# Two regions in DRAM for the second layer's experts, and scatters without a wait between tiles

## Chip, cores and metric

The kernel runs on one core of one Trainium2 chip. The metric is the device time of one execution in microseconds (us). Several executions are timed; one further execution is recorded by the hardware profiler, and all rows here come from that one.

## What is computed

The program is a two-layer transformer on x of 16 batches x 512 tokens x 256 features in fp32. Each layer scales and shifts a normalised x, adds an attention branch, and then a branch with experts. The change is in the last part, the experts of the second layer (`_L1_ffn_ref`):

```python
def _moe(x, gate_w, w1, w2):            # T = 8192 tokens, 8 experts, top 2
    probs = jax.nn.sigmoid(x_flat @ gate_w)
    _, sel = jax.lax.top_k(probs, TOP_K)
    w_topk = jnp.take_along_axis(probs, sel, axis=1)
    w_topk = w_topk / (jnp.sum(w_topk, axis=-1, keepdims=True) + 1e-06)
    ...  # each (token, choice) gets a slot in its expert, up to a capacity of 2560
    h = jax.nn.gelu(jnp.einsum('ecd,edf->ecf', padded_x, w1), approximate=False)
    out_padded = jnp.einsum('ecf,efd->ecd', h, w2)...
    out_w = out_rep * w_topk.reshape(-1)[:, None]
    return out_w.reshape(T, TOP_K, D).sum(axis=1).reshape(B, S, D)

src = _rmsnorm(x + _gqa(x, ...), norm1_w)
src = src + _moe(src, gate_w, w1, w2)
return _rmsnorm(src, norm2_w)           # times a gate, added to x, is the output
```

## The kernel before

The program is one long sequence of blocks: set-up, the first layer's attention (`local_attention_block`), its experts on two batches' rows (`routed_experts_block`), the second layer's attention and routing (`mixer_block`), and the second layer's experts (`experts_block`). Each block has one instruction list per engine, and semaphores set the order. SyncE issues nearly all DMAs from one in-order list, so whatever waits there holds back every later load and store. GpSimd issues the indirect DMAs (scatters) from its own list.

Ahead of `experts_block`, `mixer_block` has written the normalised rows `src` to DRAM (`src_dram`, 8192 rows of 256; the profile calls it src_rows) and has scattered a copy of each row, with its two routing entries, into the slots of its experts (`padded_dram`). A row there is 260 numbers: 256 features, the token's number (column D), the slot of its first choice (D+1), and the two weights.

`experts_block` then works through 71 tiles (NTILEX) of 256 rows, each with one expert. Per tile i:

- SyncE loads the rows xe (260 KB), w1 and w2 (512 KB each), the weights three tiles ahead of their use, each as soon as the tile that holds the buffer is through with it (`up_done`, `y_done`).
- TensorE, iteration i: transposes of tile i+2 (L4135), up-projection of tile i+1 (L4147), down-projection of tile i (L4159). Each projection is 16 matmuls. The up-projection waits for VectorE's copy of the transposed rows.
- ScalarE applies gelu.
- VectorE, iteration i, in this order: `copy_rows(i+2)` (L4040) copies the transposed rows out of PSUM; `place_rows(i)` waits until the scatters of tile i-3 have landed, since they read the same buffer of `place`, then makes the row numbers `place` (L4049) and the weights (L4052 to L4059); in some iterations a step of a finished batch; `copy_out(i)` (L4065) writes the weighted output rows `ye`. The instructions run in order, so a wait in `place_rows(i)` holds back `copy_out(i)` and `copy_rows(i+3)`.
- GpSimd issues two indirect DMAs (L4013), 128 rows each, that add `ye` into `src_dram` at `place`. Ahead of the first it waits until both scatters of tile i-1 have landed, since a token's two choices may lie in neighbouring tiles and would be added to the same row. The second also waits for `up_done` of tile i+2.

The tiles are sorted so that batch b is complete after tile 4b+10. With it, in the iterations that follow: SyncE loads its 512 rows back (`load_src`, L3946; for the last batch in two halves, L3950) at i = 4b+12; VectorE takes statistics (`stats`, L4078) at i = 4b+13, the reciprocal square root (`root`, many small steps of 128x4) at 4b+14, scales by gate and norm (`scale`, L4092) at 4b+15; GpSimd adds the result to x (`add_x`, L4001) after the scatters of tiles 4b+15 and 4b+16; SyncE stores x (`store`, L3956) at i = 4b+18. The last batch is finished on VectorE alone (L4118, L4125).

Parts of `padded_dram` are zero-filled in the first layer's attention, by stores of SyncE, two for each batch (`clear`, L758).

Of the kernel before, what the change touches and what calls it, by code (L numbers as in the profile page):

```python
# [5 lines left out]
F32 = mybir.dt.float32  # L6
# [4 lines left out]
ALU = mybir.AluOpType  # L11
AX = mybir.AxisListType

P = 128
D = 256
C = D // P
B = 16
S = 512
NT = S // P
T = B * S  # L20
# [620 lines left out]
        sp.dma_start(m.n1w[:, :], I["L1_ffn_norm1_w"].partition_broadcast(P)).then_inc(m.mixer_w_in, 16)  # L641


def local_attention_block(nc, m, I, mods_dram, padded_dram, sorted_dram):

# [5 lines left out]
    with nc.cleanup_on_exit(), ctx:  # L651
        def sem(name):
# [24 lines left out]

        expert_norm = (m.xn_rows[:, :, :], kT[:, 0, :, :].rearrange("p c s -> p (c s)")[:, 0:NT * ROW]
                       .rearrange("p (t d) -> p t d", d=ROW))
        ZERO_STORES = 2 * B + 1 + (NTILE0 + ZR - 1) // ZR  # L680
# [50 lines left out]
        def _(sp):  # L731
# [23 lines left out]
            def clear(b):  # L755

                for j in range(2):
                    sp.dma_start(padded_dram[bass.ds(b * (E * CAP // B) + j * (P * ZR), P * ZR), :]  # L758
                                 .rearrange("(p r) d -> p (r d)", p=P), no_rows).then_inc(zero_filled, 16)

            sp.wait_ge(m.rows_out, 16)
            load_norm_rows(0)
# [3090 lines left out]
def experts_block(nc, m, I, mods_dram, src_dram, padded_dram, out):  # L3853
# [10 lines left out]
    with nc.cleanup_on_exit(), ctx:  # L3864
# [12 lines left out]
        src = sb("src_e", [P, 2, NT, D])  # L3877
        second = sb("second", [P, RT])
        change = sb("change", [P, RT])
        weight = sb("weight", [P, WB, RT])  # L3880
# [26 lines left out]
            return m.x[:, b * (NT * D) + h * (2 * D):b * (NT * D) + (h + 1) * (2 * D)]  # L3907

        def pair(b, h):
            return src[:, b % 2, 2 * h:2 * h + 2, :].rearrange("p t d -> p (t d)")  # L3910

        block = ctx.enter_context(nc.Block())

# [1 line left out]
        def _(sp):  # L3915
# [26 lines left out]
            def load_src(b):  # L3942
                rows_sent(complete(b))
                if b >= 2:
                    sp.wait_ge(x_ready, 2 * (b - 1))
                sp.dma_start(src[:, b % 2, :, :], src_dram[b * S:(b + 1) * S, :].rearrange("(t p) d -> p t d", p=P))\  # L3946
                    .then_inc(src_in[b % 2], 16)

            def load_last(b, h):
                sp.dma_start(src[:, b % 2, 2 * h:2 * h + 2, :],  # L3950
                             src_dram[b * S + h * (2 * P):b * S + (h + 1) * (2 * P), :].rearrange("(t p) d -> p t d", p=P))\
                    .then_inc(src_in[h], 16)

            def store(b, h):
                sp.wait_ge(x_ready, 2 * b + h + 1)
# [41 lines left out]
        @block.gpsimd  # L3997
        def _(pool):
            def add_x(b, h):
                pool.wait_ge(z_ready, b * NT + 2 * h + 2)  # L4000
                pool.tensor_tensor(x_half(b, h), x_half(b, h), pair(b, h), ALU.add).then_inc(x_ready, 1)  # L4001

            for i in range(NTILEX):
                pool.wait_ge(place_ready, i + 1)
                pool.wait_ge(ye_ready, i + 1)
                for t in range(RT):
                    if t == 0 and i:

                        pool.wait_ge(sent[(i - 1) % WB], 16 * RT * ((i - 1) // WB + 1))

                    if t == 1 and i + 2 < NTILEX:
                        pool.wait_ge(up_done, 2 * (i + 2) + 1)
                    pool.indirect_dma_start(src_dram,  # L4013
                                            bass.IndirectOffsetOnAxis(ap=place[:, i % WB, t:t + 1], axis=0),
                                            ye[:, i % WB, t, :], None, bounds_check=T - 1, oob_is_err=False,
                                            compute_op=ALU.add)\
                        .then_inc(sent[i % WB], 16)
                if i >= 15 and i % 4 in (3, 0):
                    add_x((i - 15) // 4, (i - 15) % 4)
            for h in range(2):  # L4020
# [13 lines left out]
        def _(dve):  # L4034
# [8 lines left out]
            def place_rows(i):  # L4043
                u = i % WB
                dve.wait_ge(x_in[u], 16 * (i // WB) + 16)

                if i >= WB:
                    dve.wait_ge(sent[u], 16 * RT * (i // WB))
                dve.tensor_copy(place[:, u, :], xe[:, i % XB, :, D]).then_inc(place_ready, 1)  # L4049

                dve.wait_ge(weight_ready, 4 * i)
                dve.scalar_tensor_tensor(out=second[:, :], in0=xe[:, i % XB, :, D + 1], scalar=m.row_x[:, i:i + 1],  # L4052
                                         in1=m.own[:, :], op0=ALU.subtract, op1=ALU.not_equal).then_inc(weight_ready, 1)
                dve.tensor_tensor(change[:, :], xe[:, i % XB, :, D + 3], xe[:, i % XB, :, D + 2], ALU.subtract)\
                    .then_inc(weight_ready, 1)
                dve.wait_ge(weight_ready, 4 * i + 2)
                dve.tensor_tensor(change[:, :], change[:, :], second[:, :], ALU.mult).then_inc(weight_ready, 1)
                dve.wait_ge(weight_ready, 4 * i + 3)
                dve.tensor_tensor(weight[:, u, :], change[:, :], xe[:, i % XB, :, D + 2], ALU.add).then_inc(weight_ready, 1)  # L4059
# [13 lines left out]
                dve.tensor_tensor(gate_norm[:, b, :], gate_norm[:, b, :], n2w[:, :], ALU.mult).then_inc(gates_ready, 1)  # L4073

            def stats(b):
                dve.wait_ge(src_in[b % 2], 16 * (b // 2) + 16)
                for t in range(NT):
                    step(dve.bn_stats(m.bn[:, t, :], src[:, b % 2, t, :]))  # L4078

            def root():  # L4080
                step.settle()
# [7 lines left out]
                emit_rsqrt(dve, step, m, m.rstd[:, 0:NT], m.meanvar[:, 0:NT, 1], EPS_NORM, NT)  # L4089

            def scale(b, t, done):
                done(dve.scalar_tensor_tensor(out=src[:, b % 2, t, :], in0=src[:, b % 2, t, :], scalar=m.rstd[:, t:t + 1],  # L4092
                                              in1=gate_norm[:, b, :], op0=ALU.mult, op1=ALU.mult))

            def scaled(ins):
# [17 lines left out]
                copy_out(i)  # L4113
            for t in range(NT):
                scale(B - 2, t, scaled)
            for t in range(NT):
                dve.wait_ge(src_in[t // 2], 16 * (B // 2 + 1 - t // 2))
                step(dve.bn_stats(m.bn[:, t, :], src[:, (B - 1) % 2, t, :]))  # L4118
            root()
            dve.wait_ge(x_ready, 2 * (B - 1))  # L4120
            for h in range(2):
# [52 lines left out]
def build_program(nc, I, out):  # L4174
# [6 lines left out]
    src_dram = nc.dram_tensor("src_rows", (T, D), F32, kind="Internal").ap()  # L4181
    ctx = ExitStack()
    with ctx:
        m = allocate(nc, ctx)
        with ExitStack() as lists:
            with ExitStack() as mixer:
                with ExitStack() as experts:
                    first_layer_lists(nc, m, experts)
                    with ExitStack() as local:
                        local_weights(nc, m, local)  # L4190
                        setup_block(nc, m, I, mods_dram)
                        expert_buffers(nc, m, experts)
                        local_attention_block(nc, m, I, mods_dram, padded_dram, sorted_dram)
# [28 lines left out]
```

## Time and profile before

| | us |
|---|---|
| median of 3 runs | 3264.03 |
| lowest, highest | 3258.34, 3270.96 |
| the profiled execution | 3275.82 |
| its span on the core | 3274.1 |

```profile
PE 3027.8 (92%) x20262; PEld 1870.4 (57%) x20262; DVE 2182.0 (67%) x6629; ACT 1589.0 (49%) x3518; POOL 1203.4 (37%) x1522
```

This line of the page gives each engine's busy time, its share of the span, and its instructions: PE is TensorE's matmuls, PEld its weight loads, DVE VectorE, ACT ScalarE, POOL GpSimd; SP or SPq is SyncE with its queue. Busy shares are averages over stages with different limits, so the stage of the change has to be read by itself: which engine is busy without a gap, and where one has gaps, what ended each wait. In a timeline a row gives the start, the time busy, the engine, the line of the kernel, what it wrote from what, and in brackets how long the engine had been idle before it and who released it.

### The profile page before, as it was taken

To read this page: it belongs to the slowest core of one execution; us is meant where nothing else is said; L and a number is where in the kernel's file an instruction comes from. 1 tells how busy PE (TensorE), PEld (TensorE's weight loads), DVE (VectorE), ACT (ScalarE), POOL (GpSimd) and SP (SyncE) were. 2 spreads that over 40 slices of the span, in tenths; PEclk is the share of its full clock that TensorE was granted. 3 is DMA by queue.
4 is the path that set the end of the run, shared out by engine and by line. 5 is a ranking of instruction groups with operands and counts; after the bars stand their busy time and mean duration, and the time that the engine had idled before them with its cause. 6 is when DMAs were issued, how large, how long until landed. Compare 5 with 4: busy or idle time off the path is not lost. (4 is left out here: it accounts for less than half of the span.)

```text
span 3274.1 us, 59846 instructions
## 1 busy us (share of the span) xinstructions
PE 3027.8 (92%) x20262; PEld 1870.4 (57%) x20262; DVE 2182.0 (67%) x6629; ACT 1589.0 (49%) x3518; POOL 1203.4 (37%) x1522
## 2 busy tenths in 40 slices
PE   6799999999998986999999999999998859998896
PEld 3566667667665653344444444444443348887785
DVE  6777777777762224788888888888887633544445
ACT  3466565565641113566667677676665511111110
POOL 2123232232333114234444444444443224444445
PEclk8899999999999997899999999999999979999998
DMA  8110010100125961122222222222222138878884
GB/s 272 5 49 27 26 50 26 50 25 26 50 68 168 310 210 48 54 62 74 75 75 75 74 74 74 75 76 76 76 75 71 52 102 218 246 212 230 225 219 131
DMA packets 269401, 338.17 MB, mean 103 GB/s; under 512 B 43952, under 2 KB 218659, under 8 KB 269105
## 3 DMA queue, kind: packets, MB, share of 16 engines
q1 hardware_dynamic: 240112, 296.62, 28.7%
q0 software_dynamic: 28464, 34.71, 5.3%
q8 instruction: 170, 2.79, 0.4%
q10 hardware_dynamic: 544, 3.15, 0.3%
q14 instruction: 111, 0.90, 0.1%
HBM read 225.77 MB, written 113.95 MB: 104 GB/s over the span
## 5 line engine op out<-in xcount | busy, mean ns | idle before, releaser
L2841 DVE TENSOR_REDUCE negmax<-psum 128x1 f32<-128x512 f32 x1024 | 667.6, 683 | 163.1 <-PE psum L3394 149.5
L2459 ACT ACTIVATE pT<-psum 128x512 f32<-128x512 f32 x1024 | 576.1, 595 | 291.7 <-PE psum L3423 199.9
L3394 PE MATMUL psum<-k_stack,q_stack 96*128 96x512 bf16 x1024 | 359.1, 389 | 20.8 <-DVE negmax L2841 17.9
L3423 PE MATMUL psum<-q_stack,k_stack 99*128 99x512 bf16 x1024 | 361.4, 384 | 15.9 <-ACT pT L2459 9.8
L4013 POOL DMA_INDIRECT src_rows<-ye,place x142 | 224.6, 1582 | 329.6 <-DVE place L4049 178.3
L4030 ACT ACTIVATE actT_x<-psum 128x512 f32<-128x512 f32 x142 | 84.8, 597 | 480.9 <-PE psum L4147 467.9
L940 ACT ACTIVATE probs<-probs,negmax 128x256 f32<-128x256 f32 x512 | 252.8, 495 | 123.4 <-DVE negmax L1031 121.8
L4147 PE MATMUL psum<-xT_x,w_x 128*128 128x256 f32 x1136 | 266.3, 389 | 30.9 <-DVE xT_x L4040 30.3
L3437 PE MATMUL psum<-pT,v_tile 128*32 128x512 f32 x2048 | 269.5, 610 | 1.0 <-ACT pT L2459 1.0
L4159 PE MATMUL psum<-w_x,actT_x 128*128 128x256 f32 x1136 | 256.6, 379 | 0.0
L4147 PEld LDWEIGHTS psum<-xT_x,w_x 128*128 128x128 f32 x1136 | 215.9, 195 | 62.7 <-DVE xT_x L4040 34.5
L1031 DVE CUSTOM_DVE_ANT_0 probs<-psum,band_mask 128x256 f32<-128x256 f32 x512 | 181.4, 420 | 104.7 <-PE psum L1304 104.0
L849 POOL TENSOR_TENSOR x<-x,scaled 128x256 f32 (+1 forms) x64 | 46.7, 729 | 525.4 <-DVE scaled L1092 525.4
L4159 PEld LDWEIGHTS psum<-w_x,actT_x 128*128 128x128 f32 x1136 | 215.8, 190 | 29.3
L1368 PE MATMUL psum<-w,actT 128*128 128x256 f32 x1024 | 231.4, 379 | 1.3 <-ACT actT L957 0.8
L1362 PE MATMUL psum<-x2T,w 128*128 128x512 f32 x512 | 228.9, 601 | 1.0 <-DVE x2T L1082 1.0
L3394 PEld LDWEIGHTS psum<-k_stack,q_stack 96*128 96x128 bf16 x1024 | 97.4, 98 | 210.6 <-DVE negmax L2841 130.9
L3423 PEld LDWEIGHTS psum<-q_stack,k_stack 99*128 99x128 bf16 x1024 | 99.3, 98 | 198.9 <-ACT pT L2459 107.2
L1368 PEld LDWEIGHTS psum<-w,actT 128*128 128x128 f32 x1024 | 193.1, 190 | 33.6 <-issue 6.2
L1362 PEld LDWEIGHTS psum<-x2T,w 128*128 128x128 f32 x512 | 99.3, 194 | 113.3 <-issue 110.0
L2272 POOL DMA_INDIRECT padded<-src,scatter_idx x128 | 125.4, 980 | 93.2 <-DVE scatter_idx L2987 56.5
L957 ACT ACTIVATE actT<-psum,b 128x512 f32<-128x512 f32 x128 | 87.9, 687 | 133.5 <-PE psum L1362 133.5
(402 smaller groups left out, 5588.3 us busy)
## 6 DMA issues: line engine op xcount, KB each, us to landing
w_x<-in_L_ffn_w_dram SPq DMA_DIRECT2D x142, 512.0 KB
w_e<-in_L_ffn_w_dram SPq DMA_DIRECT2D x46, 1024.0 KB, 7.0
q_stacks<-q_part SPq DMA_DIRECT2D x192, 128.0 KB
q_stack<-q_stacks SPq DMA_DIRECT2D x64, 384.0 KB, 4.4
padded<-w_e SPq DMA_DIRECT2D x32, 650.0 KB, 6.2
xe<-padded SPq DMA_DIRECT2D x71, 260.0 KB
gate_rows<-mods SPq DMA_DIRECT2D x66, 256.0 KB, 3.4
x<-in_L_attn_x_dram SPq DMA_DIRECT2D x16, 512.0 KB, 8.3
```

The costliest lines, as they stand in the source:

```text
L940: ins = act.activation(probs[:, h, :], probs[:, h, :], ACT.Exp, bias=negmax[:, h:h + 1], scale=-1.0, accum_out=zsum[:, t % 2, h:h + 1])
L1031: ins = dve.tensor_tensor_reduce(probs[:, h, :], bank(m, j)[:, i * 2 * P:(i + 1) * 2 * P], m.band_mask[:, variant, :], scale=-1.0, scalar= ...
L1362: mm = pe.matmul(bank(m, at), m.w1_0[:, c, f * P:(f + 1) * P], x2T[:, c, :], start=(c == 0), stop=(c == C - 1))
L1368: mm = pe.matmul(bank(m, at)[:, 0:D], actT[:, f, t * P:(t + 1) * P], m.w2_0[:, f, :], start=(f == 0), stop=(f == NF0 - 1))
L2459: act.activation(pT[:, 4 * (s % 2) + r, :], bank(m, 2 + n % 2), ACT.Exp, scale=float(DHQ) ** -0.5)\
L2841: dve.tensor_reduce(negmax[:, p // REP, h:h + 1], bank(m, max_bank(b, 16 * g + p)), AX.X, ALU.max, negate=True).then_inc(max_read, 1)
L3394: pe.matmul(bank(m, max_bank(b, 16 * g + p)), q_stack[0:K_SCORE, h, t * P:(t + 1) * P], k_stack[0:K_SCORE, g, :], start=True, stop=True).t ...
L3423: pe.matmul(bank(m, 2 + n % 2), k_stack[:, g, kc * P:(kc + 1) * P], q_stack[:, REP * g + r, :], start=True, stop=True).then_inc(sT_done, 1)
L3437: mm = pe.matmul(bank(m, VB)[VW * r:VW * (r + 1), :], v_tile[:, par, kc, g, :], pT[:, 4 * (s % 2) + r, :], start=(kc == 0), stop=(kc == NT ...
L4013: pool.indirect_dma_start(src_dram, bass.IndirectOffsetOnAxis(ap=place[:, i % WB, t:t + 1], axis=0), ye[:, i % WB, t, :], None, bounds_che ...
L4147: mm = pe.matmul(bank(m, 2 * (i % 2) + h)[:, (f % 2) * ROWS_X:(f % 2 + 1) * ROWS_X], w1[:, i % WB, c, f * P:(f + 1) * P], xT[:, i % 2, c, ...
L4159: mm = pe.matmul(bank(m, 4 + i % 2)[:, t * D:(t + 1) * D], actT[:, i % 2, f, t * P:(t + 1) * P], w2[:, i % WB, f, :], start=(f == 0), stop ...
```

## The change

- `src_dram` gets 2 x 8192 rows. The upper half takes the second choices. It is zero-filled in the first layer's attention by one more store per batch in `clear` (512 rows, 512 KB), and the count that readers of the zeros wait for (`ZERO_STORES`) grows by 16.
- `place` is now the token's number plus 8192 where this slot is not that of the first choice. It is made by a multiply-add on VectorE after `second`, in place of a copy ahead of it.
- No row of either half gets more than one addition, and GpSimd's wait between the scatters of successive tiles is taken out. The wait for `up_done` ahead of the second scatter stays, and so does that of `place_rows(i)` for tile i-3.
- `load_src` and `load_last` load both halves, so each load becomes two DMAs of the former size; the buffer `src` doubles.
- `stats` first adds the second half to the first (two additions of 128x512 per batch), also for the last batch.

```diff
@@ local_attention_block: clear @@
                 for j in range(2):
                     sp.dma_start(padded_dram[...], no_rows).then_inc(zero_filled, 16)
+                sp.dma_start(src_dram[bass.ds(b * S + T, S), :].rearrange("(p r) d -> p r d", p=P),
+                             no_rows.rearrange("p (r d) -> p r d", d=ROW)[:, 0:NT, 0:D]).then_inc(zero_filled, 16)
@@ experts_block: SyncE, load_src @@
                 rows_sent(complete(b))
                 if b >= 2:
                     sp.wait_ge(x_ready, 2 * (b - 1))
-                sp.dma_start(src[:, b % 2, :, :], src_dram[b * S:(b + 1) * S, :].rearrange("(t p) d -> p t d", p=P))\
-                    .then_inc(src_in[b % 2], 16)
+                for k in range(TOPK):
+                    sp.dma_start(src[:, b % 2, k, :, :],
+                                 src_dram[k * T + b * S:k * T + (b + 1) * S, :].rearrange("(t p) d -> p t d", p=P))\
+                        .then_inc(src_in[b % 2], 16)
@@ experts_block: GpSimd @@
                 for t in range(RT):
-                    if t == 0 and i:
-
-                        pool.wait_ge(sent[(i - 1) % WB], 16 * RT * ((i - 1) // WB + 1))
-
                     if t == 1 and i + 2 < NTILEX:
                         pool.wait_ge(up_done, 2 * (i + 2) + 1)
                     pool.indirect_dma_start(src_dram,
                                             bass.IndirectOffsetOnAxis(ap=place[:, i % WB, t:t + 1], axis=0),
-                                            ye[:, i % WB, t, :], None, bounds_check=T - 1, oob_is_err=False,
+                                            ye[:, i % WB, t, :], None, bounds_check=TOPK * T - 1, oob_is_err=False,
                                             compute_op=ALU.add)\
@@ experts_block: VectorE, place_rows @@
                     dve.wait_ge(sent[u], 16 * RT * (i // WB))
-                dve.tensor_copy(place[:, u, :], xe[:, i % XB, :, D]).then_inc(place_ready, 1)
-
                 dve.wait_ge(weight_ready, 4 * i)
...
                 dve.wait_ge(weight_ready, 4 * i + 2)
+                dve.scalar_tensor_tensor(out=place[:, u, :], in0=second[:, :], scalar=float(T), in1=xe[:, i % XB, :, D],
+                                         op0=ALU.mult, op1=ALU.add).then_inc(place_ready, 1)
@@ experts_block: VectorE, stats @@
-                dve.wait_ge(src_in[b % 2], 16 * (b // 2) + 16)
+                dve.wait_ge(src_in[b % 2], 16 * TOPK * (b // 2 + 1))
+                for h in range(2):
+                    step(dve.tensor_tensor(pair(b, h), pair(b, h), src[:, b % 2, 1, 2 * h:2 * h + 2, :]
+                                           .rearrange("p t d -> p (t d)"), ALU.add))
+                step.settle()
@@ experts_block: VectorE, last batch @@
-            for t in range(NT):
-                dve.wait_ge(src_in[t // 2], 16 * (B // 2 + 1 - t // 2))
-                step(dve.bn_stats(m.bn[:, t, :], src[:, (B - 1) % 2, t, :]))
+            for h in range(2):
+                dve.wait_ge(src_in[h], 16 * TOPK * (B // 2 + 1 - h))
+                step(dve.tensor_tensor(pair(B - 1, h), pair(B - 1, h), src[:, (B - 1) % 2, 1, 2 * h:2 * h + 2, :]
+                                       .rearrange("p t d -> p (t d)"), ALU.add))
+                step.settle()
+                for t in (2 * h, 2 * h + 1):
+                    step(dve.bn_stats(m.bn[:, t, :], src[:, (B - 1) % 2, 0, t, :]))
```

## Rows read from the trace of the kernel before

**Rows 1.** Windows of the experts' stage: us, busy of each engine, PEclk, DMA share, GB/s.
```profile
2693.80:2892.40 198.60, 198.60 (x976) 174.97 (x975) 81.41 (x311) 32.25 (x54) 85.71 (x56) 1.00 0.86 230
2892.40:3245.20 352.80, 321.94 (x1523) 278.81 (x1521) 174.24 (x618) 50.15 (x84) 165.01 (x108) 0.98 0.78 213
3245.20:3274.10 28.90, 0.02 (x1) 0.00 (x0) 14.24 (x51) 0.00 (x0) 12.82 (x9) 0.55 0.23 73
```

**Rows 2.** Timeline of TensorE: start us, us, engine line op, tiles, count, [idle before].
```profile
2690.33 3.62 PE L4159 MATMUL psum<-w_x,actT_x 128*128 128x256 f32 x16
...
2841.14 3.62 PE L4147 MATMUL psum<-xT_x,w_x 128*128 128x256 f32 x16
...
2848.48 3.62 PE L4147 MATMUL psum<-xT_x,w_x 128*128 128x256 f32 x16
...
2928.00 6.56 PE L4147 MATMUL psum<-xT_x,w_x 128*128 128x256 f32 x16 [3.42 <-DVE xT_x L4040]
...
3238.15 7.07 PE L4159 MATMUL psum<-w_x,actT_x 128*128 128x256 f32 x32
```

**Rows 3.** Waits, 2700 to 3240: engine line waited for: us in total, times, longest.
```profile
DVE place L4049 <- DMA src_rows<-ye,place: 144.6, 35, 6.3
...
PE psum L4147 <- DVE xT_x L4040: 30.3, 14, 3.7
```

**Rows 4.** Timeline of GpSimd in a stalled stretch.
```profile
2923.99 1.83 POOL L4001 TENSOR_TENSOR x<-x,src_e 128x512 f32<-128x512 f32 x1
...
2929.40 1.81 POOL L4013 DMA_INDIRECT src_rows<-ye,place  x1 [0.30 <-issue]
2939.28 1.55 POOL L4013 DMA_INDIRECT src_rows<-ye,place  x1 [8.07 <-issue]
2941.14 1.55 POOL L4013 DMA_INDIRECT src_rows<-ye,place  x1 [0.30 <-issue]
```

**Rows 5.** Timeline of VectorE in the same stretch.
```profile
2923.41 2.44 DVE L203 SCALAR_TENSOR_TENSOR rstd<-newton,rstd 128x4 f32<-128x4 f32 x1
...
2937.83 0.17 DVE L4049 CAST place<-xe 128x2 uint32<-128x2 f32 x1 [6.26 <-DMA src_rows<-ye,place]
...
2944.95 0.17 DVE L4049 CAST place<-xe 128x2 uint32<-128x2 f32 x1 [4.78 <-DMA src_rows<-ye,place]
```

**Rows 6.** Waits of the queue of SyncE, 2700 to 3240.
```profile
SPq L3956 <- POOL x L4001: 83.6, 12, 9.4
```

**Rows 7.** Timeline around the load of batch 2, without stalls.
```profile
2842.00 0.37 SPq L3946 DMA_DIRECT2D src_e<-src_rows  x1
...
2849.31 1.41 DVE L4078 BATCH_NORM_STATS2 bn<-src_e 128x6 f32<-128x256 f32 x4 [6.28 <-DMA src_e<-src_rows]
...
2851.41 0.68 DVE L4040 COPY xT_x<-psum 128x512 f32<-128x512 f32 x1
```

**Rows 8.** Chain that ended last: start us, us, what.
```profile
3257.85 2.71 DMA src_rows<-ye,place
...
3260.61 2.69 DMA src_e<-src_rows
...
3268.69 0.69 DVE x L4125
```

**Rows 9.** DMA in 40 equal slices of 2693.8 to 2892.4.
```profile
GB/s 174 211 267 221 157 272 175 227 245 234 178 243 227 216 219 202 235 204 223 329 204 288 163 213 213 330 204 280 277 160 222 353 178 320 255 165 152 282 309 194
```

**Rows 10.** Groups of instructions, 2700 to 3240: line, engine, op, shapes, count, busy, mean ns.
```profile
L4052 DVE SCALAR_TENSOR_TENSOR second<-xe,row_x,own_x 128x2 f32<-128x2 f32 x68 | 14.7, 216 | 0.0
```

**Rows 11.** Timeline of GpSimd at the end of the first layer's attention.
```profile
943.25 2.78 POOL L857 TENSOR_TENSOR xn<-xn,gate_rows 128x256 f32<-128x256 f32 x4 [25.46 <-DMA gate_rows<-mods]
...
971.30 0.73 POOL L849 TENSOR_TENSOR x<-x,scaled 128x256 f32<-128x256 f32 x1 [4.75 <-DVE scaled L1092]
```

**Rows 12.** Timeline around the last tile.
```profile
3250.45 0.88 DVE L4065 TENSOR_SCALAR ye<-psum,weight 128x256 f32<-128x256 f32 x2
...
3255.99 1.55 POOL L4013 DMA_INDIRECT src_rows<-ye,place  x1 [1.97 <-DMA src_rows<-ye,place]
```

More of the change, by code:

```diff
@@ L641, in load_mixer_weights, with local_attention_block @@
         sp.dma_start(m.n1w[:, :], I["L1_ffn_norm1_w"].partition_broadcast(P)).then_inc(m.mixer_w_in, 16)
-def local_attention_block(nc, m, I, mods_dram, padded_dram, sorted_dram):
+def local_attention_block(nc, m, I, mods_dram, padded_dram, sorted_dram, src_dram):
     ctx = ExitStack()
@@ L679, in local_attention_block @@
                        .rearrange("p (t d) -> p t d", d=ROW))
-        ZERO_STORES = 2 * B + 1 + (NTILE0 + ZR - 1) // ZR
+        ZERO_STORES = 2 * B + 1 + (NTILE0 + ZR - 1) // ZR + B
         second_s = sem("a_second_modulation_steps")
@@ L3876, in experts_block @@
         gate_norm = sb("gate_norm", [P, B, D])
-        src = sb("src_e", [P, 2, NT, D])
+        src = sb("src_e", [P, 2, TOPK, NT, D])
         second = sb("second", [P, RT])
@@ L3909, in pair @@
         def pair(b, h):
-            return src[:, b % 2, 2 * h:2 * h + 2, :].rearrange("p t d -> p (t d)")
+            return src[:, b % 2, 0, 2 * h:2 * h + 2, :].rearrange("p t d -> p (t d)")
         block = ctx.enter_context(nc.Block())
@@ L3945, in load_src @@
                     sp.wait_ge(x_ready, 2 * (b - 1))
-                sp.dma_start(src[:, b % 2, :, :], src_dram[b * S:(b + 1) * S, :].rearrange("(t p) d -> p t d", p=P))\
-                    .then_inc(src_in[b % 2], 16)
+                for k in range(TOPK):
+                    sp.dma_start(src[:, b % 2, k, :, :],
+                                 src_dram[k * T + b * S:k * T + (b + 1) * S, :].rearrange("(t p) d -> p t d", p=P))\
+                        .then_inc(src_in[b % 2], 16)
             def load_last(b, h):
-                sp.dma_start(src[:, b % 2, 2 * h:2 * h + 2, :],
-                             src_dram[b * S + h * (2 * P):b * S + (h + 1) * (2 * P), :].rearrange("(t p) d -> p t d", p=P))\
-                    .then_inc(src_in[h], 16)
+                for k in range(TOPK):
+                    at = k * T + b * S + h * (2 * P)
+                    sp.dma_start(src[:, b % 2, k, 2 * h:2 * h + 2, :],
+                                 src_dram[at:at + 2 * P, :].rearrange("(t p) d -> p t d", p=P)).then_inc(src_in[h], 16)
             def store(b, h):
@@ L4075, in stats @@
             def stats(b):
-                dve.wait_ge(src_in[b % 2], 16 * (b // 2) + 16)
+                dve.wait_ge(src_in[b % 2], 16 * TOPK * (b // 2 + 1))
[3 more added lines that the diff above has]
+                step.settle()
                 for t in range(NT):
-                    step(dve.bn_stats(m.bn[:, t, :], src[:, b % 2, t, :]))
+                    step(dve.bn_stats(m.bn[:, t, :], src[:, b % 2, 0, t, :]))
             def root():
@@ L4091, in scale @@
             def scale(b, t, done):
-                done(dve.scalar_tensor_tensor(out=src[:, b % 2, t, :], in0=src[:, b % 2, t, :], scalar=m.rstd[:, t:t + 1],
+                done(dve.scalar_tensor_tensor(out=src[:, b % 2, 0, t, :], in0=src[:, b % 2, 0, t, :], scalar=m.rstd[:, t:t + 1],
                                               in1=gate_norm[:, b, :], op0=ALU.mult, op1=ALU.mult))
@@ L4180, in build_program @@
     chosen_out0 = nc.dram_tensor("chosen_out0", (ROWS_MOE0 * TOPK, D), F32, kind="Internal").ap()
-    src_dram = nc.dram_tensor("src_rows", (T, D), F32, kind="Internal").ap()
+    src_dram = nc.dram_tensor("src_rows", (TOPK * T, D), F32, kind="Internal").ap()
     ctx = ExitStack()
@@ L4192, in build_program @@
                         expert_buffers(nc, m, experts)
-                        local_attention_block(nc, m, I, mods_dram, padded_dram, sorted_dram)
+                        local_attention_block(nc, m, I, mods_dram, padded_dram, sorted_dram, src_dram)
                     routing_lists(nc, m, lists)
```

## The prediction

> **What bounds the kernel now.** I first read the table of busy time by stage. The second layer's experts run from 2690 to 3245 us and split in two. Up to 2892.4 TensorE is busy all of the 198.6 us, 27 tiles at 7.36 us; after that it is busy 321.9 of 352.8 us, 30.9 idle [rows 1]. The timeline of TensorE gives the unstalled period again: the up-projections of two successive tiles start 7.34 us apart, and I use 7.35. The down-projections of tiles 0 and 69 start 547.8 us apart, while 69 periods less one missing set of transposes (0.44, the gap from a transpose to its up-projection) make 506.7. So the stalls cost 41.1 us: 30.9 of idle time and some 10 of late or slow matmuls. One group of 16 matmuls behind a stall took 6.56 instead of 3.62 us [rows 2].
>
> Then the waits: TensorE waits for VectorE's copy of transposed rows (L4040), and VectorE's own largest wait is L4049, `place`, for a scatter of src_rows: 144.6 us in 35 waits [rows 3]. The timeline shows how that comes about. GpSimd issues a tile's two scatters, waits until both have landed, then issues the next tile's. The second scatter of one tile is issued at 2929.40 and the next tile's first at 2939.28, 9.9 us later [rows 4]; `place`, which needs the scatter of three tiles back, is let go at 2937.83 and 2944.95, 8.4 and 3.8 us after the scatter's issue [rows 4, 5]. Add the 1.85 us between the two scatters, and twice in four tiles an addition of 1.83 us, and this chain's period lies near or over 7.35 us. GpSimd falls behind until it is three tiles late; from there VectorE waits in `place` with its copies queued behind, and TensorE follows. So in the second part the scatter chain bounds the kernel, in the first TensorE.
>
> **The change, part by part.** (1) The wait on the previous tile's scatters is removed. GpSimd's work per tile is then two scatters, 1.85 + 1.55 + some 0.3, and half an addition, 0.9: 4.6 us of 7.35 [rows 4]. A tile's scatter follows its own rows by about a microsecond, and `place` three tiles later asks for it some 15 us (two periods) after those rows were ready. Taken off that are 3.7 us of issue and 8.4 of landing at the worst [rows 4, 5]; it still fits. All 41.1 us go if nothing else is late.
>
> SyncE gains as well: the store of a finished batch waited 83.6 us for GpSimd's additions, with the next tiles' loads queued behind it [rows 6]. No wait of TensorE hung on those, so I count nothing.
>
> (2) What is late next is the load of a finished batch. It becomes two loads of 512 KB (0.524 MB), and VectorE adds the halves before its statistics. The case closest to the future is load 2 of before, in the unstalled part: issued 2842.00, statistics begin 2849.31, the copy queued behind ends 2851.41 + 0.68 = 2852.09. The up-projection that needs this copy starts one period after that of 2848.48, at 2855.8: 3.7 us of slack [rows 2, 7]. The change takes of it two additions of 0.69 each (the same shape stands at the end of the kernel) [rows 8], 1.4 us, and the transfer of 0.524 MB behind 0.5 MB of weights: at the stretch's mean of 230 GB/s 2.3 us [rows 1], at the fastest fortieth (353 GB/s) 1.5, at the slowest (152) 3.4 [rows 9]. So 3.7 - 1.4 - 2.3 leaves 0.0, with +0.8 and -1.1 as ends. Per batch a loss of 0 to 1.1 us, 15 batches: 0 to 17 us; I take +5, as half of the draws should lie on the side that costs nothing. Each such shift also delays the square-root steps of the next tile. These get shorter, though: today GpSimd's late addition holds one of them for 2.44 us [rows 4, 5], and with GpSimd in time that addition falls into a gap of VectorE.
>
> (3) `place` becomes a multiply-add (0.22 us [rows 10]) behind two other small steps, some 0.4 us later in its tile. GpSimd waits for the tile's rows anyway, which come after it. 0; if that cover were gone, 0.4 on VectorE per stalled tile.
>
> (4) Sixteen more stores of zeros (0.524 MB each) in the first layer's attention, one per batch. SyncE waits tens of microseconds between batches there. Two places are tight. At about 57 us two of them go ahead of the second layer's modulation rows, which are read only in the second layer. At 936 us the last one goes ahead of the row load that GpSimd waits for until 943.25: at 230 GB/s 2.3 us more. GpSimd is idle 4.75 us before 971.30 and absorbs that [rows 11]. 0, at most +2.3.
>
> (5) The end. From the last down-projection (3238.15 + 7.07 = 3245.2 [rows 2]) to the last scatter pass 12.6 us. Of these, the last tile's rows are ready at 3250.45 + 0.88 = 3251.3, yet its first scatter is issued at 3255.99: 4.7 us of waiting for the tile before, of which some 0.3 remain, -4.4 [rows 12]. New on that path: the issue of one more load ahead of the first statistics (0.37) and two additions of 0.69, +1.8 [rows 7, 8]. Sum -2.6, and with less backlog of VectorE ahead of it -3; ends -4.5 and 0.
>
> Sum: -41.1 + 5 - 3 = -39. The profiled execution took 3275.8 us (span 3274.1 and 1.7 around it), so it would be 3237. It lies 11.8 us over the median of 3264.0, and over all three of the timed runs; stalls that hang on landing times may differ between executions. Against the median: 3225 us.
>
> **Rivals.** A: the doubled load is on the path in every batch. For it: the margin above is 0.0. Then 15 x 1.1 = 17 us, and some stalls are followed by slow matmuls at 2.9 us each [rows 2]; with two of them 23 instead of 5: 3243.
>
> B: the new additions are held up by GpSimd. Today one small VectorE step took 2.44 us and ended just when GpSimd's addition did [rows 4, 5]. If one addition per batch is held for 1.83 us beyond the slack, that is 27 us more: 3252. Against it: by (1) GpSimd is through with its addition some 5 us ahead of the load's landing. The Trainium skill (SBUF — State Buffer, section "Who interferes with whom") says that a VectorE instruction with two SBUF inputs contends with a GpSimd instruction that reads SBUF, and that the second to issue is blocked until the first is through. The new additions are of this kind; by that rule, the trace agrees in the one step named.
>
> C, the other side: the DMA queue becomes the bound. The stage moves 0.230 x 198.6 + 0.213 x 352.8 = 120.8 MB [rows 1], and 8.4 more make 129.2. Weights would come late on every tile if the queues can't sustain 129.2 MB in less time than the 551.4 us of today, that is 234 GB/s; at 220 the stage takes 587 us, and 3264 + 36 - 3 = 3297. For it: the engines' busy share is 0.86 at 230 GB/s. Against: single fortieths reach 353 [rows 9], and TensorE waited for no weights.
>
> D: the change doesn't do what it says, because consecutive scatters hold each other up in the queue or GpSimd's issue blocks; `place` then waits as before: 3260.
>
> **How the numbers follow.** Forecast 0.60, A 0.17, B 0.06, C 0.07, D 0.10. The range runs from the case with no loss at (2), the best end, and the fastest run of before as base (3258.3 - 41.1 - 4.5, about 3212; I take 3210) to between A and B, 3250. It leaves out C and D, 0.17. Faster by over 0.5% (16 us, about what a measurement can tell) means below 3247.7: forecast, A, half of B, 0.80. Within: the other half of B, D, a little of C, 0.14. Slower: 0.06.
>
> **What would show it.** TensorE is busy all through the stage, 7.35 us a tile; `place` has no wait on scatters; scatters of successive tiles start 7.35 us apart and overlap the landing of the last; SyncE's wait for x is gone. VectorE's wait for the load grows from 6.3 us to about 8.5. The end, from the last down-projection to the end of the span, shrinks from 28.9 to 26 us. If TensorE idles once per four tiles behind L4040 with VectorE waiting for src_e, A is right; if the new additions take over 1 us, B; if TensorE waits for weights, C; if `place` still waits, D.

## The result

| us | before | changed |
|---|---|---|
| median | 3265.1 (4 runs, 3258.3 to 3271.0) | 3217.2 (4 runs, 3214.1 to 3219.0) |
| profiled execution | 3275.8 | 3218.7 |
| its span | 3274.1 | 3216.9 |

The ratio is 0.9853 with a 95% interval of 0.9832 to 0.9874: 48 us faster, with 41 to 55 inside the interval. The changed kernel measured again on another occasion gave 3217.1 us, ratio 0.9863 (0.9846 to 0.9879). Forecast were 3225 us and 39 us.

The page by stage, changed kernel (the columns are those of [rows 1]):

```profile
2681.70:2880.20 198.50, 198.50 (x975) 174.84 (x974) 85.64 (x331) 32.25 (x54) 91.50 (x60) 1.00 0.90 246
2880.20:3191.80 311.60, 311.57 (x1525) 274.13 (x1523) 162.62 (x639) 50.18 (x84) 161.49 (x108) 1.00 0.88 258
3191.80:3216.90 25.10, 0.00 (x0) 0.00 (x0) 11.79 (x40) 0.00 (x0) 7.50 (x6) 0.58 0.28 84
```

TensorE now has no gap in either stretch: the second is 311.6 us long where it was 352.8, with 311.57 busy. The queues carry 246 and 258 GB/s in place of 230 and 213.

TensorE's timeline, the down-projections of tile 0 and of tiles 69 and 70:

```profile
2678.28 3.62 PE L4168 MATMUL psum<-w_x,actT_x 128*128 128x256 f32 x16
...
3184.70 7.07 PE L4168 MATMUL psum<-w_x,actT_x 128*128 128x256 f32 x32
```

From the start of tile 0's to that of tile 69's there are 506.4 us, where [rows 2] gave 547.8. The end, from the last down-projection (3184.70 + 7.07) to the end of the span, is 25.1 us after 28.9.

VectorE's waits and SyncE's wait for x, in 2700 to 3190:

```profile
DVE ye L4066 <- PE psum L4168: 143.1, 39, 5.2
DVE src_e L4079 <- DMA src_e<-src_rows: 95.1, 14, 7.9
```

```profile
SPq L3961 <- POOL x L4006: 12.2, 2, 7.2
```

The 144.6 us of `place` [rows 3] are gone, and so is TensorE's wait for L4040. What is left is VectorE waiting for TensorE, as it should, and 6.8 us a batch for the doubled load (about 8.5 was forecast). SyncE's wait is 12.2 instead of 83.6 us [rows 6].

GpSimd, two tiles in a row:

```profile
2793.83 1.55 POOL L4014 DMA_INDIRECT src_rows<-ye,place  x1 [1.82 <-DVE ye L4066]
2795.68 1.54 POOL L4014 DMA_INDIRECT src_rows<-ye,place  x1 [0.30 <-issue]
2796.68 1.85 POOL L4006 TENSOR_TENSOR x<-x,src_e 128x512 f32<-128x512 f32 x1
2801.18 1.57 POOL L4014 DMA_INDIRECT src_rows<-ye,place  x1 [2.65 <-DVE ye L4066]
```

The tiles' first scatters start at 2793.83 and 2801.18, 7.35 us apart, in place of the 9.9 of [rows 4], and each is released by its own rows. GpSimd is idle 2.65 us even after an addition. Issue and landing of successive tiles now overlap: in e11, the changed kernel measured again, 35 of the 70 later tiles issue their first scatter before the last one of the tile ahead has landed.

The load of batch 0, to be set beside [rows 7]:

```profile
2771.10 0.93 SPq L3949 DMA_DIRECT2D src_e<-src_rows  x2
...
2778.79 1.29 DVE L4079 TENSOR_TENSOR src_e<-src_e 128x512 f32<-128x512 f32 x2 [6.53 <-DMA src_e<-src_rows]
...
2780.12 1.40 DVE L4083 BATCH_NORM_STATS2 bn<-src_e 128x6 f32<-128x256 f32 x4
...
2782.21 0.68 DVE L4041 COPY xT_x<-psum 128x512 f32<-128x512 f32 x1
...
2785.01 2.32 PE L4156 MATMUL psum<-xT_x,w_x 128*128 128x256 f32 x10
```

The two loads are issued from 2771.10 on, the additions begin 7.7 us later and take 1.29, and the copy behind them ends at 2782.89, 2.1 us before its up-projection.

### The profile page after: what moved, and what is told of

The parts are those of the page before. It is cut to its first block and busy times, and to the rows that moved or that the text cites. A ratio compares the mean times of both kernels' runs of the same rounds, so it can differ in the third digit from the quotient of the medians.

```text
span 3216.9 us, 59942 instructions
## 1 busy us (share of the span) xinstructions
PE 3011.3 (94%) x20262; PEld 1865.6 (58%) x20262; DVE 2174.5 (68%) x6661; ACT 1588.9 (49%) x3518; POOL 1200.3 (37%) x1522
## 5 line engine op out<-in xcount | busy, mean ns | idle before, releaser
L4156 PE MATMUL psum<-xT_x,w_x 128*128 128x256 f32 x1136 | 259.3, 382 | 0.0
L4066 DVE TENSOR_SCALAR ye<-psum,weight 128x256 f32<-128x256 f32 x142 | 62.0, 478 | 159.2 <-PE psum L4168 158.7
```

The source lines that it names most:

```text
L4156: mm = pe.matmul(bank(m, 2 * (i % 2) + h)[:, (f % 2) * ROWS_X:(f % 2 + 1) * ROWS_X], w1[:, i % WB, c, f * P:(f + 1) * P], xT[:, i % 2, c, ...
```

## Experiments

Stage is the time from tile 0's to tile 69's down-projection, start that of tile 0's, end the time from the last down-projection to the end of the span; all three are from the profiled execution. e1 to e4 ran together on one chip, e5 to e8 on one where the kernel before took 3275.4 us, and e9 to e12 together on another occasion. Times are to be compared with the `before` of their own line. e3 leaves the second choices out of its result; the other kernels compute everything.

| kernel | start | stage | end | median | before | ratio (95%) |
|---|---|---|---|---|---|---|
| before | 2690.3 | 547.8 | 28.9 | | | |
| changed | 2678.3 | 506.4 | 25.1 | 3217.2 | 3265.1 | 0.9853 (0.9832 to 0.9874) |
| e1_wait_kept | 2680.1 | 548.9 | 32.9 | 3271.2 | 3264.1 | 1.0025 (1.0015 to 1.0034) |
| e2_six_buffers | 2672.5 | 550.9 | 28.6 | 3261.5 | 3264.1 | 0.9988 (0.9973 to 1.0004) |
| e3_one_load_no_adds | 2678.9 | 506.4 | 21.3 | 3215.8 | 3264.1 | 0.9853 (0.9837 to 0.9870) |
| e4_two_more_loads | 2678.0 | 553.3 | 26.8 | 3264.9 | 3264.1 | 1.0002 (0.9992 to 1.0011) |
| e5_one_more_load | 2686.2 | 522.3 | 25.3 | 3242.6 | 3275.4 | 0.9901 (0.9880 to 0.9923) |
| e6_wait_two_back | 2691.4 | 506.4 | 25.4 | 3229.6 | 3275.4 | 0.9858 (0.9836 to 0.9879) |
| e7_zeros_twice | 2690.5 | 506.4 | 24.0 | 3230.6 | 3275.4 | 0.9867 (0.9844 to 0.9891) |
| e8_last_loads_two_queues | 2688.2 | 506.4 | 24.3 | 3228.2 | 3275.4 | 0.9857 (0.9836 to 0.9879) |
| e9_zeros_only | 2676.3 | 550.7 | 29.2 | 3262.8 | 3264.0 | 1.0007 (0.9996 to 1.0019) |
| e10_before_again | 2671.6 | 553.5 | 28.7 | 3264.7 | 3264.0 | 1.0002 (0.9991 to 1.0013) |
| e11_after_again | 2681.1 | 506.4 | 24.7 | 3217.1 | 3264.0 | 0.9863 (0.9846 to 0.9879) |
| e12_rows_earlier | 2672.4 | 506.4 | 24.3 | 3213.3 | 3264.0 | 0.9854 (0.9838 to 0.9871) |

### Is the removed wait the whole gain?

e1_wait_kept puts it back:

```diff
                 for t in range(RT):
+                    if t == 0 and i:
+                        pool.wait_ge(sent[(i - 1) % WB], 16 * RT * ((i - 1) // WB + 1))
                     if t == 1 and i + 2 < NTILEX:
```

> The changed kernel with one part undone: GpSimd again waits for the previous tile's scatters to land; two regions, doubled loads, additions and extra zeros stay. Theory (the removed wait is the whole gain): GpSimd falls three tiles behind again, VectorE waits in place for some 140 us or more, TensorE loses 41 us or a little more in the stage since the doubled loads now meet a late VectorE: 3258 to 3278 us, against 3217 of the changed kernel. Rival (the gain comes from another part, such as fewer additions to rows that another scatter has just touched, since first and second choices now lie in different regions): landings get shorter, 3217 to 3235 us.

It took 3271.2 us, inside the first range. The waits in 2700 to 3190:

```profile
DVE second L4053 <- issue: 103.8, 29, 5.9
DVE src_e L4081 <- DMA src_e<-src_rows: 67.3, 13, 8.0
...
PE psum L4158 <- DVE xT_x L4043: 14.6, 10, 2.6
```

VectorE again waits 103.8 us at the head of `place_rows` (the page shows no releaser; the wait there is the one for the scatter of three tiles back), and TensorE waits for the copy of transposed rows. TensorE also waits 6.1 us for tiles' rows (xe). The stage is 548.9 us. So regions, loads, additions and zeros give nothing by themselves. They cost something: ratio 1.0025, with the end 4 us longer than in the kernel before. A kernel before with only the wait left out, and both choices still added into one region, was not run (its sums could be wrong). So it is not shown whether the second region does more for the time than make the removal possible.

### Is it the chain, or only that VectorE stands in its way?

e2_six_buffers is the kernel before with `ye`, `place` and `weight` six deep:

```diff
+    YB = 6
...
-                if i >= WB:
-                    dve.wait_ge(sent[u], 16 * RT * (i // WB))
+                if i >= YB:
+                    dve.wait_ge(sent[i % WB], 16 * RT * ((i - YB) // WB + 1))
```

> The kernel before with six instead of three buffers for ye, place and weight, so that VectorE need not wait for the scatter of three tiles back but of six. One region and GpSimd's wait between tiles stay. Theory (the chain of scatter and landing is itself slower than TensorE's 7.35 us a tile): the backlog only grows larger, then SyncE's wait for a batch's scatters and VectorE's wait for its load take over, and the end gets longer: 3245 to 3265 us. Rival (it was only that VectorE stood in place's wait; the chain would keep up): 3217 to 3230 us.

3261.5 us, in the theory's range, with no difference that can be told from the kernel before. Its waits in 2700 to 3190:

```profile
DVE bn L4080 <- DMA src_e<-src_rows: 138.7, 13, 14.1
...
POOL src_rows L4014 <- DMA src_rows<-ye,place: 115.1, 25, 7.8
...
PE psum L4149 <- DVE xT_x L4041: 16.9, 9, 2.3
```

`place` is gone from the list and the stage is still 550.9 us. GpSimd waits 115.1 us for landings as such, and VectorE now stands before the statistics for 138.7 us: SyncE may load a batch only when its scatters have landed. The tiles took 8.0 us on average (550.9 / 69), where TensorE needs 7.34. The chain on GpSimd is too slow, and more buffers only choose who waits for it. This was the theory's account, and the rival is out.

e6_wait_two_back asks how much overlap is needed:

```diff
+                    if t == 0 and i >= 2:
+                        pool.wait_ge(sent[(i - 2) % WB], 16 * RT * ((i - 2) // WB + 1))
```

> The changed kernel, but GpSimd waits, ahead of tile i's scatters, until those of tile i-2 have landed. One landing may then be open. Theory (only the serial chain issue, landing, issue was the bound; the landing lasts under 9 us and two periods are 14.7): no loss, stage 506 us, 3214 to 3221 us. Rival (many scatters need to be open at once): TensorE idles again, over 3225 us.

The stage is 506.4 us, as in the changed kernel, and the ratio 0.9858. (3229.6 us is over the range named, since this chip ran the kernel before some 11 us slower; 3264 us times the ratio is inside it. The same holds for e7, and to 0.3 us for e8.) One open landing is enough.

### What does the doubled load cost?

e3_one_load_no_adds leaves out the second load (`for k in range(1)`) and the additions. e5 and e4 add one and two more loads of 512 KB per batch:

```diff
+                for k in range(n):      # n = 1 in e5, 2 in e4
+                    sp.dma_start(src[:, b % 2, TOPK + k, :, :],
+                                 src_dram[b * S:(b + 1) * S, :].rearrange("(t p) d -> p t d", p=P))\
+                        .then_inc(src_in[b % 2], 16)
```

> The changed kernel without the second half's loads and the additions (the second choices are left out of the result). It measures what the doubled load costs. Theory (the load fits into VectorE's slack, and only the end pays): the stage up to the last down-projection stays at 506 us from tile 0 to tile 69, the end shrinks by 2 to 4 us: 3212 to 3216 us. Rival A of the prediction (the load is on the path in every batch): 3195 to 3205 us.

> The changed kernel with two more loads of 512 KB per batch ahead of the statistics, into buffers of their own that nobody reads. In the changed kernel the copy behind the statistics ends 2.1 us (batch 0) and 1.8 us (batch 1) before its up-projection starts. Theory (slack of about 2 us, 2.3 us for each load): VectorE's wait for the load grows from 6.8 to about 11 us, TensorE is late by 2.5 to 3 us a batch and waits for the copy of transposed rows: 3250 to 3265 us. Rival C (the DMA queues have a limit near today's 255 GB/s): TensorE waits for weights as well and the time goes over 3280 us. Rival (more slack than that): under 3230 us.

> The changed kernel with one more load of 512 KB per batch into a buffer that nobody reads. Two more loads cost 46.9 us in the stage, 3.1 a batch. If a load costs 2.3 us and the slack is 1.8 to 2.1 us, one more load leaves TensorE late by 0.2 to 0.5 us a batch: stage 509 to 514 us from tile 0 to tile 69, time 3219 to 3227 us. Rival (no slack to speak of, half of what two loads cost): stage 530 us, time 3240 us.

Batch 0 of e3:

```profile
2771.67 0.38 SPq L3949 DMA_DIRECT2D src_e<-src_rows  x1
...
2777.68 1.41 DVE L4079 BATCH_NORM_STATS2 bn<-src_e 128x6 f32<-128x256 f32 x4 [4.85 <-DMA src_e<-src_rows]
...
2779.78 0.68 DVE L4041 COPY xT_x<-psum 128x512 f32<-128x512 f32 x1
...
2785.58 1.68 PE L4149 MATMUL psum<-xT_x,w_x 128*128 128x256 f32 x7
```

Means over batches 0 to 12, from such rows:

| loads per batch | from first issue to first use | copy ends before its up-projection by | stage |
|---|---|---|---|
| 1 (e3) | 6.3 us | 4.7 us | 506.4 |
| 2 (changed) | 8.0 | 1.7 (0.8 to 2.1) | 506.4 |
| 3 (e5) | 10.8 | -1.0 | 522.3 |
| 4 (e4) | 12.1 | -2.2 | 553.3 |

A minus stands for the time that TensorE was idle for the copy. The added loads cost 1.65, 2.8 and 1.3 us. From one to two, 1.65 us of load and 1.3 of additions take the slack from 4.7 to 1.7, and the stage doesn't notice, as e3 was expected to show (3215.8 us, in its range). In e11 the slack went down to 0.4 us in one batch, and the stage was 506.4 us all the same. e4 met its range (3264.9 us), with VectorE waiting 11.0 us a batch. e5 did not: 3242.6 us on a chip that is 11 us slower, stage 522.3 where 509 to 514 was expected. That expectation failed twice over. I had read 1.8 to 2.1 us of slack from batches 0 and 1 alone, while over 13 batches it goes down to 0.8 with a mean of 1.7; and I had priced the third load at 2.3 us, while it took 2.8, about the 2.7 us (1.7 + 1.0) by which the copy slipped.

TensorE named the copy of transposed rows and never the weights in either (one wait of 0.4 us in e4 was for a tile's rows), with the queues at 259 GB/s over e4's stage. So rival C's limit near 255 is out.

### A gap that costs more than itself

In e5 12 gaps cost 12.4 us and the stage grew by 15.9, some 0.3 us more per gap than the gap itself. In e4 the 13 gaps of batches 0 to 12 cost 28.2 and two smaller ones 1.0, and it grew by 46.9. TensorE in e4, and two windows right behind this gap:

```profile
2853.25 5.41 PE L4160 MATMUL psum<-xT_x,w_x 128*128 128x256 f32 x16 [2.41 <-DVE xT_x L4045]
```

```profile
2853.20:2855.00 1.80, 1.75 (x6) 1.43 (x7) 1.63 (x13) 0.00 (x0) 1.56 (x1) 0.70 1.07 385
2855.00:2856.60 1.60, 1.60 (x5) 1.27 (x4) 1.32 (x9) 0.16 (x1) 1.30 (x1) 0.50 1.03 313
```

And in e5 the same batch:

```profile
2855.05 3.72 PE L4160 MATMUL psum<-xT_x,w_x 128*128 128x256 f32 x16 [1.07 <-DVE xT_x L4045]
```

```profile
2855.10:2858.50 3.40, 3.40 (x16) 3.01 (x17) 2.96 (x21) 0.60 (x1) 2.96 (x2) 1.00 0.92 298
```

Behind 2.41 us of idleness the granted clock is 0.70 of full speed over the first 1.8 us and then 0.50, the lower of the two levels (1.2 GHz), and the 16 matmuls take 5.41 us. Behind 1.07 us it is 1.00 and they take what they always do. Of e4's 13 gaps (1.4 to 2.8 us) eight were followed by such a group, 14.3 us in all; of e5's 12 (0.4 to 2.2 us) none.

The length of the gap doesn't settle it. In e4 the clock fell behind gaps of 2.10 and 2.17 us and not behind 2.13 and 2.16, and in the kernel before the longest gap of all cost only itself, with the granted clock at 1.00 behind it:

```profile
3099.35 3.72 PE L4147 MATMUL psum<-xT_x,w_x 128*128 128x256 f32 x16 [3.73 <-DVE xT_x L4040]
```

What decides it is left open here.

### The zeros

e7_zeros_twice doubles each new store, e9_zeros_only adds the stores to the kernel before:

```diff
+                sp.dma_start(spare_dram[bass.ds(b * S, S), :].rearrange("(p r) d -> p r d", p=P),
+                             no_rows.rearrange("p (r d) -> p r d", d=ROW)[:, 0:NT, 0:D]).then_inc(zero_filled, 16)
```

> The changed kernel with each of its 16 new stores of zeros doubled (the second copy goes to rows in DRAM that nobody reads). Theory (they lie beside a queue that is nearly idle and GpSimd absorbs the delay of the last one): 0 to 2 us more, 3214 to 3221 us, and the row load that GpSimd waits for until 944.08 lands about 1 to 2 us later. Rival (each delays the modulation rows of its batch): 16 x 1 us, 3233 us.

> The kernel before with the 16 extra stores of zeros alone (to rows nobody reads). Theory (hidden): within 3 us of the kernel before, and the experts' stage starts within 3 us of where the kernel before, profiled again on this chip, starts it. Rival (the six-buffer kernel, which has no extra stores, started that stage at 2672.5 us and four kernels with them on the same chip at 2678 to 2680, so the stores cost some 6 us ahead of the stage): 5 to 7 us slower than before.

GpSimd's step behind the last store, in the changed kernel and in e7:

```profile
944.08 2.78 POOL L859 TENSOR_TENSOR xn<-xn,gate_rows 128x256 f32<-128x256 f32 x4 [27.17 <-DMA gate_rows<-mods]
```

```profile
947.53 2.79 POOL L861 TENSOR_TENSOR xn<-xn,gate_rows 128x256 f32<-128x256 f32 x4 [28.91 <-DMA gate_rows<-mods]
```

It was at 943.25 [rows 11]: 0.8 us later, then 3.4 more, over the 1 to 2 us expected of e7. Single executions scatter here too: the three without the new stores have this step at 941.2 to 943.3 (mean 942.4), the ten that have them once at 943.4 to 946.3 (mean 944.7). The ratios are 0.9867 against 0.9857 and 0.9858 for e8 and e6 on the same chip, and 1.0007 for e9. No cost can be told, and 16 x 1 us is excluded by e9's interval (up to 1.0019, 6 us). The start of the stage can't decide it. In e9 it is at 2676.3 us and in e10, below, 4.7 us earlier, where at most 3 were expected; but equal code ahead of the stage varies by more (2671.6 and 2690.3 for the kernel before). On both chips that profiled an execution without the new stores beside others with them, the one without starts its stage first (e2 2672.5 against 2678.0 to 2680.1; e10 2671.6 against 2672.4 to 2681.1). A cost of a few us ahead of the stage is not excluded.

### The first profile's late start

> The kernel before once more with its profile, on the same chip as the next. Its first profile started the experts' stage 12 us later than that of the changed kernel. Theory (chance of the one execution, since nothing in the change can shorten the stages ahead of it): its stage starts within 4 us of the changed kernel's, it takes 545 to 550 us from tile 0 to tile 69, and the end 27 to 31 us. Rival (a real gain ahead of the stage): 10 us or more later again.

> The changed kernel once more with its profile on the same chip. Stage 506.4 us, end 24 to 25.5 us, and 45 to 49 us faster than before.

```profile
2671.61 3.62 PE L4159 MATMUL psum<-w_x,actT_x 128*128 128x256 f32 x16
...
3225.06 7.07 PE L4159 MATMUL psum<-w_x,actT_x 128*128 128x256 f32 x32
```

This execution starts the stage at 2671.6, 9.5 us ahead of e11, where the first profile was 12 us behind. It is neither theory nor rival as I put them, since it leaves the 4 us on the other side; what it shows is that the start of a single execution says nothing to 10 us. The stage is longer here, 553.5 us (e9: 550.7), over the 545 to 550 expected; the end, 28.7 us, is as expected. e11 met all of its expectation: stage 506.4 us, end 24.7, and 46.9 us faster (3217.1 against 3264.0).

### The end, and rows loaded earlier

e8_last_loads_two_queues moves the second choices' two loads of the last batch to ScalarE's queue; e12_rows_earlier has this too and loads tile 1's rows ahead of tile 0's second weights:

```diff
+            act.wait_ge(x_ready, 2 * (B - 2))       # e8, behind a wait for all scatters
+            for h in range(2):
+                at = T + (B - 1) * S + h * (2 * P)
+                act.dma_start(src[:, (B - 1) % 2, 1, 2 * h:2 * h + 2, :], src_dram[at:at + 2 * P, :]...)
...
             load_rows(0)                            # e12
             load_up(0, e)
+            load_rows(1)
             load_down(0, e)
```

> The changed kernel with the last batch's four loads split: the first choices' two on SyncE, the second choices' two on ScalarE, which is idle by then. In the changed kernel SyncE issues the four within 1.92 us, and the last lands 5.2 us after its issue. Theory (the issue is on the path, the transfer of 1 MB is shared anyway): the end from the last down-projection to the end of the span goes from 25.1 to about 24 us, time 3215 to 3217 us, a difference that only the trace shows. Rival (the landing is bound by the transfer alone): the end stays at 25.1 us.

> The changed kernel with the last batch's loads on two queues and, at the start of the experts' stage, tile 1's rows loaded ahead of tile 0's second weights. In the changed kernel TensorE waits 3.4 us for these rows with 1 MB of weights ahead of them. Theory: the first down-projection starts 1.5 to 2.5 us sooner after the first transposes (15.2 us in the changed kernel), and the end is up to 1 us shorter: 2 to 3 us faster than the changed kernel, hardly to be told in the times. Rival (tile 0's first weights, not the rows, are what the first up-projection really waits for): no gain at the start.

The chain that ended last, changed kernel and e8:

```profile
3196.65 2.72 DMA src_rows<-ye,place
...
3199.42 0.38 SPq L3956
...
3200.86 5.23 DMA src_e<-src_rows
...
3206.11 0.70 DVE src_e L4123
```

```profile
3206.58 2.72 DMA src_rows<-ye,place
...
3209.36 4.42 DMA src_e<-src_rows
...
3213.80 0.70 DVE src_e L4130
```

In the changed kernel 6.7 us pass from the first issue (3199.42) to the last load's landing (3206.09); the issues lie in them. In e8 the first half's landing, 4.4 us after its issue, releases VectorE, and the second half is no longer waited for. But the end is 24.3 us, and e7, with the changed kernel's own code there, had 24.0. The ends of the five executions with that code lie between 24.0 and 25.4, so e8 is inconclusive.

The start of e12, and of the changed kernel:

```profile
2659.84 1.11 PE L4157 MATMUL psum<-ident,xe 128*128 128x128 f32 x4 [12.66 <-DMA xe<-padded]
2662.90 1.12 PE L4157 MATMUL psum<-ident,xe 128*128 128x128 f32 x4 [1.94 <-DMA xe<-padded]
...
2672.38 3.62 PE L4181 MATMUL psum<-w_x,actT_x 128*128 128x256 f32 x16
```

```profile
2663.10 1.11 PE L4144 MATMUL psum<-ident,xe 128*128 128x128 f32 x4 [12.65 <-DMA xe<-padded]
2667.66 1.11 PE L4144 MATMUL psum<-ident,xe 128*128 128x128 f32 x4 [3.44 <-DMA xe<-padded]
```

TensorE waits 1.94 instead of 3.44 us for the second tile's rows, its first up-projection takes 4.85 instead of 5.98 us, and tile 0's down-projection starts 12.5 instead of 15.2 us after the first transposes (14.9 in e11, and 13.7 to 15.9 in the 13 executions without this change). Its rival is out. Median 3213.3 us (3211.9 to 3214.3) against 3217.1 (3215.3 to 3221.0) for e11 at the same time: the runs don't overlap, though the two ratios' intervals do. It has the lowest median of this study, but its ratio of 0.9854 can't be told from the 0.9853 of the changed kernel's first measurement.

## The prediction, step by step

**The sum.** The time came out at 3217, in the range and 8 us under the forecast; 48 us were gained where 39 were forecast. Two slips in the working bear on nothing here: the range up to 3250 leaves out B's 3252 too, not C and D alone, and of the 15 batches loaded in the stage only 14 have a copy of transposed rows queued behind their statistics.

**(1) The wait.** Right in mechanism and place. The 41.1 us were one execution's; e9, with the same chain, and e10, the same kernel, had 550.7 and 553.5 us of stage, so the stage gains 41 to 47 us against 506.4. e1 shows that nothing else brings it, e2 that the chain and not the buffer was at fault, e6 that one open landing is enough. That GpSimd needs 4.6 of 7.35 us a tile holds too: a scatter starts with its rows.

**(2) The doubled load: the term that was mis-sized.** I took +5 us for the stage, and it was 0. The margin of 0.0 us was wrong by 1.7. Of this, 0.65 us is the price of the second load, 1.65 instead of the 2.3 us that its bytes take at the mean rate. That rate is a fair price all the same: the three added loads cost 1.65, 2.8 and 1.3 us, 1.9 on average, so a single one is known to some 0.9 us, and a margin of 0.0 was never more exact than that. The larger part, 1.0, is the slack before the load: I took the slowest of three loads (3.7 us), while without second load and additions it is 4.7 on average. The additions were as priced (1.29 us in all). Two more loads did bring what A described, so A was a matter of size: about 1.7 us a batch away. A's 2.9 us for a slow group was the worst of three in the kernel before; the other two, and all eight of e4, lost 1.8.

**(3) `place`.** 0.20 us, with no waiting. In 2700 to 3190:

```profile
L4056 DVE SCALAR_TENSOR_TENSOR place<-second,xe 128x2 uint32<-128x2 f32 x67 | 13.4, 200 | 2.3
...
L203 DVE SCALAR_TENSOR_TENSOR rstd<-newton,rstd 128x4 f32<-128x4 f32 x42 | 6.8, 162 | 1.4
```

The second of these rows answers B. The same group in the kernel before:

```profile
L203 DVE SCALAR_TENSOR_TENSOR rstd<-newton,rstd 128x4 f32<-128x4 f32 x36 | 26.5, 735 | 1.2
```

The steps of L203 took 735 ns on average with GpSimd's late additions beside them and 162 ns now. Of the 36 of before nine took some 2.45 us, each beside such an addition, and ended 0.03 us after it; the statistics (one input, 0.41 us each) were not held by such additions; in the changed kernel no instruction of VectorE ran beside an addition of GpSimd in this window. The additions of the change took 0.69 us each in all 30 cases. The Trainium skill (SBUF — State Buffer, section "Who interferes with whom") has it that the second to issue waits until the first is through. The trace agrees on the waiting, but not plainly on the order: the nine held steps have recorded starts 0.58 us ahead of GpSimd's. One of the new additions did meet GpSimd, in e4:

```profile
3232.62 1.86 POOL L4010 TENSOR_TENSOR x<-x,src_e 128x512 f32<-128x512 f32 x1
3233.36 2.29 DVE L4083 TENSOR_TENSOR src_e<-src_e 128x512 f32<-128x512 f32 x2 [3.77 <-DMA src_e<-src_rows]
```

The two took 2.29 us in place of 1.29, so B's mechanism exists. It cost nothing in the changed kernel: once GpSimd is in time, its addition falls beside an idle VectorE.

**(4) The zeros.** 0 was forecast, at most +2.3. GpSimd's step came 0.8 us later in the changed kernel and 2.3 us later on average over the executions named above; no cost in the time shows in e7 or e9, to within e9's interval.

**(5) The end.** -3 was forecast, and -3.8 was measured (-4.0 with e10 and e11), from two terms that were each too small. That the sum came close is luck. Around the last tile:

```profile
3192.85 0.88 DVE L4066 TENSOR_SCALAR ye<-psum,weight 128x256 f32<-128x256 f32 x2
...
3194.57 1.77 POOL L4014 DMA_INDIRECT src_rows<-ye,place  x1 [0.79 <-DVE ye L4066]
```

From the end of the last down-projection to the first scatter there are 2.8 us (3191.77 to 3194.57), where there were 10.8 (3245.2 to 3255.99 [rows 12]): -8.0, not -4.4. I had counted GpSimd's wait and only 0.4 us for VectorE. VectorE was 4 us late with the last rows, since the last but one batch's steps stood ahead of them; one of these small steps took 2.40 us beside an addition of GpSimd (3247.75, 1.85 us):

```profile
3247.24 2.40 DVE L201 TENSOR_TENSOR newton<-newton,var_eps 128x4 f32<-128x4 f32 x1
```

Against that, the doubled load costs 3.8 us by e3 (25.1 less 21.3, one execution each, where equal code gave ends 1.4 us apart), not 1.8: the last piece lands 5.2 us after its issue, in place of 2.7 [rows 8].

**C and D.** Excluded: the queues gave 259 GB/s in e4 without a wait for weights, and scatters of successive tiles do overlap (35 of 70 in e11).

**What remains.** Stage and end give 41 to 47 and 4 us, 45 to 51 together, and 48 were measured. What the start of the stage adds or takes is within its own spread of up to 19 us between two executions of the kernel before.

## To carry to other kernels

A wait for a landing between the links of a serial chain puts the landing into every period: here tiles took 7.9 us on average (547.8 / 69) where TensorE needed 7.34. Where a second destination let two links be open at once, that cost was gone, and more buffers behind the chain didn't replace it. Before a transfer is called free, measure the slack of the instruction that is queued behind its reader, over all occurrences and not the first two or three, and don't take the bytes over the mean rate for exact: here it said 2.3 us, and three such loads took 1.65, 2.8 and 1.3. Here the change had 1.7 us of slack left per batch; one more load of the same size took a third of the gain, and two took all of it.

## What was not expected of the hardware

A gap of TensorE of 2.4 us was followed by the clock at the lower level and 1.8 us of loss on top, a gap of 1.1 us by none, and one of 3.73 us by none either. In e4 such groups are 14.3 of the 46.9 us that the stage grew by. And a scatter that lands in 2.7 us at the quiet end (from its issue) needed 5.9 us in the median and up to 8.5 amid the stage's loads, over the 96 scatters of the changed kernel whose landing the trace has. The Trainium skill (DMA: Bandwidth & Descriptors, section "Anatomy of one DMA — SWDGE (gpsimd) path") gives a fixed cost of about 2 us, mostly the receipt of the write. The trace has little more than that in the quiet, and two to three times its own quiet figure under load, which is what a chain of such waits has to be priced with.
